# Expert results fetched and added on GpSimd inside the linear attention; scores of the gated heads in row groups

## The reference, cut to what matters

```
layer 0:  x += causal attention(16 heads of 64)
          x += cross attention(16 heads of 64, dense mask)
          t  = rmsnorm(layernorm(x)) * norm_weight
          x += layernorm(x) + sum over a token's two best of 8 experts of w_e * FFN_e(t)
layer 1:  x += linear attention: q, k = elu(qW)+1, elu(kW)+1; (sum of past k v^T) q / (sum of past k) q
          x += cross attention(16 heads of 16)
          x += gated heads:
               gates = sigmoid(x w_gate); of 8 experts per head only the best is kept (gm)
               values = einsum(gm, value_experts, x)
               out = softmax(causal(q k^T / 8)) values
               out = einsum(gm, output_experts, out), summed over 8 heads of 64
```

## Time and profile before

| | |
|---|---|
| median of 3 runs | 4053.97 us (4052.62 to 4055.01) |
| the profiled execution | 4053.33 us |
| its span, first to last instruction | 4051.5 us |
| TensorE busy | 3628.1 us (90%) |
| VectorE busy | 2985.8 us (74%) |
| ScalarE busy | 2128.6 us (53%) |
| GpSimd busy | 192.3 us (5%) |
| granted TensorE clock, mean | 0.956 of full speed |

### The profile page before, as it was taken

The page is one execution under the profiler, slowest core; times in us unless marked ns, Lnnn a source line. Parts: engine busy times, 40 slices in busy tenths (PEclk is TensorE's granted clock), DMA queues, the critical chain, the costliest instruction groups (busy, mean ns, idle before and its releaser), DMA issues. The chain is left out here.

```text
span 4051.5 us, 93201 instructions
## 1 busy us (share of the span) xinstructions
PE 3628.1 (90%) x28994; PEld 3057.7 (75%) x28994; DVE 2985.8 (74%) x9270; ACT 2128.6 (53%) x6632; POOL 192.3 (5%) x254
## 2 busy tenths in 40 slices
PE   6999999899999997099548879998799999999998
PEld 5888888688888887089436656665688888888887
DVE  5666666677777775556568868888888888888886
ACT  5777777677777773145213337776433333333333
POOL 0000000000000000611430000000000000000000
PEclk9999999899999996599879989999899999999999
DMA  2000000100000002522210000000200000000000
GB/s 96 0 0 0 0 0 0 58 11 10 11 15 10 10 6 99 171 72 77 78 52 0 0 19 21 19 17 16 93 13 13 10 10 13 8 10 13 10 11 9
DMA packets 56111, 109.74 MB, mean 27 GB/s; under 512 B 8368, under 2 KB 27184, under 8 KB 55728
## 3 DMA queue, kind: packets, MB, share of 16 engines
q1 hardware_dynamic: 46656, 80.72, 6.3%
q0 software_dynamic: 8464, 26.22, 2.0%
q10 hardware_dynamic: 864, 1.19, 0.1%
HBM read 72.46 MB, written 35.65 MB: 27 GB/s over the span
## 5 line engine op out<-in xcount | busy, mean ns | idle before, releaser
L637 ACT ACTIVATE c_pr<-c_sm,c_nmx 128x256 f32<-128x256 f32 x512 | 254.6, 499 | 153.6 <-DVE c_nmx L483 153.6
L2248 ACT CAST f_zgT<-f_ps_g 128x512 fp32r<-128x512 f32 x256 | 150.9, 590 | 319.7 <-PE f_ps_g L1977 319.7
L127 PE MATMUL f_ps_out<-f_out_rounded,f_zgT 128*128 128x256 f32 x1024 | 309.7, 302 | 0.0
L128 PE MATMUL f_ps_out<-f_out_rest,f_zgT 128*128 128x256 f32 x1024 | 287.9, 281 | 0.0
L129 PE MATMUL f_ps_out<-f_out_rounded,f_zgT 128*128 128x256 f32 x1024 | 287.6, 281 | 0.0
L637 ACT ACTIVATE a_pr<-a_sm,a_nmx 128x128 f32<-128x128 f32 (+1 forms) x512 | 227.1, 444 | 107.0 <-DVE a_nmx L483 107.0
L483 DVE CUSTOM_DVE_ANT_0 a_sm<-a_ps_s,causal 128x128 f32<-128x128 f32 (+1 forms) x512 | 152.6, 354 | 165.9 <-PE a_ps_s L369 165.9
L2097 DVE TENSOR_REDUCE f_v<-f_gv 128x64 f32<-128x512 f32 x256 | 269.3, 1052 | 0.4
L1700 ACT ACTIVATE c_pr<-c_ps_s,c_nmx 128x256 f32<-128x256 f32 x512 | 214.3, 500 | 89.7 <-DVE c_nmx L1551 89.7
L483 DVE CUSTOM_DVE_ANT_0 c_sm<-c_ps_s,c_mask 128x256 f32<-128x256 f32 x512 | 186.8, 421 | 92.1 <-PE c_ps_s L369 90.5
L2088 DVE TENSOR_TENSOR f_gv<-f_ps_v,f_gm_step 128x512 f32<-128x512 f32 x256 | 175.5, 686 | 97.9 <-PE f_ps_v L129 86.4
(11 more groups left out here) (368 smaller groups left out, 11309.3 us busy)
## 6 DMA issues: line engine op xcount, KB each, us to landing
f_slot_rows<-f_run POOLq DMA_DIRECT2D x1, 9216.0 KB, 34.9
f_rows<-f_slot_rows SPq DMA_DIRECT2D x72, 128.0 KB, 2.1
f_slot_out<-f_y SPq DMA_DIRECT2D x72, 128.0 KB, 1.9
c_ctx_stage<-in_ctxT SPq DMA_DIRECT2D x32, 256.0 KB, 2.8
small<-in_f_w SPq DMA_DIRECT2D x16, 512.0 KB, 3.9
x_sb<-in_x SPq DMA_DIRECT2D x8, 512.0 KB, 8.4
small<-in_c_w SPq DMA_DIRECT2D x8, 512.0 KB, 3.9
c_mask_stage<-in_mask SPq DMA_DIRECT2D x16, 256.0 KB, 3.0
```

Of the source, the lines that this page charges most:

```text
L127: nc.tensor.matmul(out, sh, mh, start=start, stop=False, **kw)
L128: nc.tensor.matmul(out, sh, ml, start=False, stop=False, **kw)
L637: last = nc.scalar.activation(pr[:, r, i, 0:n], sm[:, j, i, 0:n], ACT.Exp, bias=nmx[:, j, i:i + 1], scale=-1.0, accum_out=sums[:, r, i:i + 1])
```

## The change

Three things are changed. First, the gathers, the weighted additions and the statistics leave the end of the experts' block. In the linear attention GpSimd now fetches the results of one batch with four indirect DMAs, scales each with its weights and adds it to x, with eight operations of its own, batch by batch. VectorE measures batch b + 1 at the start of the first step of batch b, into small tiles of its own; ScalarE takes the root of that batch alone behind `apart` in that step, and then one exponential of a single column; VectorE inverts it ahead of `normalise(b + 1)`. The weights `wt` and the row numbers `slot_at` are kept beyond the experts' block. Second, the part below zero is taken by ScalarE as a Relu of the negative, ahead of its exponential, and `low_part` is gone. Third, in the gated heads q is scaled once, and the scores of the two heads of a step are products of 64 rows each, one in the upper and one in the lower half of the rows, alternating. They go to two banks, of which the second is `ps_qk`, the one of the projection, since all eight are in use. Both heads' scores now come at k = 1, the row maxima and exponentials at k = 1 and 2, the scaling at k = 2 and 3; `project` and the turn of x also wait for the maxima.

```diff
--- before.py
+++ after.py
...
-        wt = sb("wt", [P, TOPS, TILES])
-        slot_at = sb("slot_at", [P, TOPS, TILES], U32)
+        wt, slot_at = c.wt, c.slot_at
...
-        back = sb("back", [P, RR, TOPS, D])
...
-            all_stored(pool)
-            for n in range(TILES):
-                if n >= RR:
-                    pool.wait_ge(summed, n - RR + 1)
-                for r in range(TOPS):
-                    pool.indirect_dma_start(back[:, n % RR, r, :], None, c.y.rearrange("n p d -> (n p) d"),
-                                            bass.IndirectOffsetOnAxis(ap=slot_at[:, r, n:n + 1], axis=0)).then_inc(gathered[n % RR], 16)
...
-                nc.vector.tensor_scalar(xt(n), xt(n), grow[:, n:n + 1], move[:, n:n + 1], ALU.mult, ALU.subtract).then_inc(grown, 1)
+                nc.vector.tensor_scalar(xt(n), xt(n), grow[:, n:n + 1], move[:, n:n + 1], ALU.mult, ALU.subtract)
...
-            for n in range(TILES):
-                dve.wait_ge(gathered[n % RR], 16 * TOPS * (n // RR + 1))
-                dve.wait_ge(grown, n + 1)
-                nc.vector.scalar_tensor_tensor(xt(n), back[:, n % RR, 0, :], wt[:, 0, n:n + 1], xt(n), ALU.mult, ALU.add).then_inc(half_sum, 1)
-                dve.wait_ge(half_sum, n + 1)
-                nc.vector.scalar_tensor_tensor(xt(n), back[:, n % RR, 1, :], wt[:, 1, n:n + 1], xt(n), ALU.mult, ALU.add).then_inc(summed, 1)
-                if n % ST == ST - 1:
-                    dve.wait_ge(summed, n + 1)
-                    batch_stats(nc, dve, c, stats, n // ST)
...
+            fetched = sb("fetched", [P, ST, TOPS, D])
+            bn_in = sb("bn_in", [P, ST, 6])
+            mv_in = sb("mv_in", [P, ST, 2])
+            spare = sb("spare", [P, 1])
...
+                def fetch(b):
+                    for i in range(ST):
+                        if b:
+                            pool.wait_ge(summed, ST * (b - 1) + i + 1)
+                        for r in range(TOPS):
+                            pool.indirect_dma_start(fetched[:, i, r, :], None, c.y.rearrange("n p d -> (n p) d"),
+                                                    bass.IndirectOffsetOnAxis(ap=c.slot_at[:, r, b * ST + i:b * ST + i + 1], axis=0)
+                                                    ).then_inc(gathered[i], 16)
...
+                def add_experts(b):
...
+                    for i in range(ST):
+                        n = b * ST + i
+                        xt = c.x[:, n, :]
+                        pool.wait_ge(gathered[i], 16 * TOPS * (b + 1))
+                        for r in range(TOPS):
+                            nc.gpsimd.tensor_scalar(fetched[:, i, r, :], fetched[:, i, r, :], c.wt[:, r, n:n + 1], None,
+                                                    ALU.mult).then_inc(weighted, 1)
+                        pool.wait_ge(weighted, TOPS * n + 1)
+                        nc.gpsimd.tensor_tensor(xt, xt, fetched[:, i, 0, :], ALU.add).then_inc(half_sum, 1)
+                        pool.wait_ge(weighted, TOPS * n + 2)
+                        pool.wait_ge(half_sum, n + 1)
+                        nc.gpsimd.tensor_tensor(xt, xt, fetched[:, i, 1, :], ALU.add).then_inc(summed, 1)
+                for b in range(B):
+                    fetch(b)
+                    add_experts(b)
...
+            if softmax:
+                dve.wait_ge(root, 1)
+                nc.vector.reciprocal(rstd[:], rstd[:]).then_inc(root, 1)
+                dve.wait_ge(root, 2)
...
+            def measure(b):
+                dve.wait_ge(summed, ST * b + ST)
+                batch_stats(nc, dve, c, stats_in, b, bn_in, mv_in)
+            def invert(b):
+                at = rstd[:, bass.ds(b * ST, ST)]
+                dve.wait_ge(rooted, b + 1)
+                nc.vector.reciprocal(at, at).then_inc(inverted, 1)
             def normalise(b):
+                if not softmax:
+                    dve.wait_ge(inverted, b + 1)
...
-            def low_part(g, s, b):
-                n = 2 * b + s // 2
-                dve.wait_ge(proj, n + 1)
-                if late(g, 1):
-                    dve.wait_ge(qk_ready, n)
-                nc.vector.tensor_scalar(low[:], ps_p[:], 0.0, None, ALU.min).then_inc(phi_s, 1)
...
-                    if now and s % 2 == 0:
-                        low_part(*now)
+                    if s == 0 and (not isinstance(b, int) or b + 1 < B):
+                        measure(b + 1)
                     if ended:
                         finish(*ended)
                     for j in range(J):
...
                     if s == 3:
                         new_stats(b - 2)
                 if s == 1 and (not isinstance(b, int) or b + 1 < B):
+                    if not softmax:
+                        invert(b + 1)
                     normalise(b + 1)
+            if not softmax:
+                measure(0)
+                invert(0)
             normalise(0)
...
+            if softmax:
+                nc.scalar.activation(rstd[:], c.mv[:, :, 1:2].rearrange("p a d -> p (a d)"), ACT.Sqrt,
+                                     bias=c.eps[:]).then_inc(root, 1)
...
+            def take_root(b):
+                act.wait_ge(stats_in, 3 * b + 3)
+                nc.scalar.activation(rstd[:, bass.ds(b * ST, ST)],
+                                     c.mv[:, bass.ds(b * ST, ST), 1:2].rearrange("p a d -> p (a d)"), ACT.Sqrt,
+                                     bias=c.eps[:]).then_inc(rooted, 1)
+                nc.scalar.activation(spare[:], c.eps[:], ACT.Exp)
...
                 else:
+                    act.wait_ge(proj, n + 1)
+                    if late(g, 1):
+                        act.wait_ge(qk_ready, n)
+                    nc.scalar.activation(low[:], ps_p[:], ACT.Relu, scale=-1.0).then_inc(phi_s, 1)
                     act.wait_ge(phi_s, 2 * n + 1)
-                    nc.scalar.activation(low[:], low[:], ACT.Exp).then_inc(phi_s, 1)
+                    nc.scalar.activation(low[:], low[:], ACT.Exp, scale=-1.0).then_inc(phi_s, 1)
...
                 if not softmax and now:
                     apart(*now)
+                if not softmax and s == 0 and (not isinstance(b, int) or b + 1 < B):
+                    take_root(b + 1)
...
+            if not softmax:
+                take_root(0)
             take_xT(0)
             run_steps(act, STEPS, slot, LAST)
...
+        ps_s = [ps_s, ps_qk]
...
                 if late(b, 1):
                     pe.wait_ge(q_ready, STEPS * b)
+                    pe.wait_ge(maxed, 2 * STEPS * b - 2)
...
             def project(g, s):
                 if late(g, 1):
                     pe.wait_ge(q_ready, g)
+                if late(g, 2):
+                    pe.wait_ge(maxed, 2 * g - 2)
...
-            def scores(g, s, j):
-                pe.wait_ge(q_ready, g + 1)
-                if late(g, 1) or j:
-                    pe.wait_ge(maxed, 2 * g + j)
+            def scores(g, s, batches):
+                pe.wait_ge(q_ready, batches)
+                if late(g, 1):
+                    pe.wait_ge(maxed, 2 * g)
                 for i in range(ST):
-                    last = nc.tensor.matmul(ps_s[:, i * S:i * S + (i + 1) * P], qT[:, s % 2, j, i * P:(i + 1) * P],
-                                            kT[:, s % 2, 0:(i + 1) * P], start=True, stop=True)
-                last.then_inc(scored, 1)
+                    for j in range(2):
+                        rows = slice(64 * j, 64 * j + 64)
+                        last = nc.tensor.matmul(ps_s[j][:, i * S:i * S + (i + 1) * P], qT[rows, s % 2, i * P:(i + 1) * P],
+                                                kT[rows, s % 2, 0:(i + 1) * P], start=True, stop=True)
+                        if i == ST - 1:
+                            last.then_inc(scored, 1)
...
                 for k in range(K):
                     if now:
                         project_v(now[0], s, k, b)
-                    if k % 2 == 0 and one:
-                        scores(one[0], one[1], k // 2)
+                    if k == 1 and one:
+                        scores(one[0], one[1], now[0] + 1 if now else one[0] + 1)
                     if k % 2 and two:
                         turn(two[0], two[1], k // 2)
...
                         if k == 0:
                             cut_piece(now[0], s)
                         gate_v(now[0], s, k)
-                    if one and k % 2 == 0:
-                        row_max(one[0], one[1], k // 2)
+                    if one and k in (1, 2):
+                        row_max(one[0], one[1], k - 1)
                     if five:
                         rest_zgT(five[0], k)
                     if now:
                         sum_v(now[0], s, k)
-                    if one and k % 2:
-                        norm(one[0], one[1], k // 2)
+                    if one and k >= 2:
+                        norm(one[0], one[1], k - 2)
...
                 act.wait_ge(proj, g + 1)
                 if late(g, 2):
                     act.wait_ge(scored, 2 * g - 2)
```

(35 more changed lines are left out.)

11 lines of the change are left out of this document (6 added, 5 removed).

## The result

The changed kernel takes 4000.31 us (median of 4 runs, 3993.21 to 4004.44) against 4053.3 of the kernel before: a ratio of 0.987, with a 95% interval of 0.985 to 0.989. That is 53 us faster where 88 were forecast, and outside the range of 3946 to 3996. The profiled execution has a span of 4000.5 us.

The account below looks back on a forecast made before the run. Bounds: gather issue after the experts, a VectorE-TensorE loop of 19.17 us a batch in the linear attention, TensorE in the gated heads. 4051.5 - 84.5 + 12.6 + 12 - 28.2 = 3963.4 us of span, 3966 measured; range 3946 to 3996.

Parts of the forecast that it names:

- part 2: Linear attention's loop: VectorE gains the statistics and a reciprocal, loses low_part; 0.8 us a batch, +12 us over 15 batches.
- rival C: Linear attention grows more: table loads cost double (+15 us), or GpSimd slows VectorE by 10% (+14); 3981 us; chance 0.18.
- The start: Linear attention's first features come 22.5 us into the stage instead of 9.9, behind batch 1's statistics: 12.6 us given back.
- I take 0.6 for each of the eight: GpSimd's eight operations on 128x256 a batch in the linear attention: 0.6 us each, bounds 0.3 and 1.2.
- 6 us of a first call: GpSimd's first call after code is loaded takes about 6 us; one such call would add 6 us.
- The experts' end: Gathers leave the experts' block, so the linear attention starts at 1986.4 instead of 2070.9: 84.5 us off.
- Part 3: Gated heads' scores in row groups of 64: 60 steps gain 0.47 us each, 28.2 us; shared bank's waits eat nothing.
- TensorE gains 0.47 us a step: Gated heads: both heads' scores take 0.85 us a step instead of 1.32; bounds nothing and 0.66.
- The table loads: Linear attention, ScalarE's take_root: two loads of 1.28 us a batch, covered by its idle time, costed at nothing.
- B: Row groups bring nothing in the gated heads, through missing overlap or the shared bank's waits: 3994 us; chance 0.13.
- D: VectorE's extra 0.8 us vanishes in its wait, or row groups give 0.66: 3954 us, both 3943; chance 0.10.
- E: Slower: GpSimd paces the linear attention, other engines wait in measure; 4114 us at 3 us an operation; chance 0.04.

Follow-up runs that it names:

- filled_half_again: Changed kernel with five unread products a batch added on TensorE between scores and values of the first step, run again: 3978.52 us, ratio 0.982 to the kernel before.
- late_measure_again: Changed kernel with measure(b + 1) moved from ahead of finish to the first step's end, ScalarE's root behind its copy of v: 3955.78 us, run again 3956.60.
- late_no_additions_again: late_measure without GpSimd's weighting and additions, one column copied instead (experts' results missing from x), run again: 3940.84 us, ratio 0.973 to the kernel before.
- gated_only: Kernel before with only the gated heads' part of the change, scores of two heads in row groups: 4026.99 us, ratio 0.994.
- no_tables_again: Changed kernel with the root replaced by a Relu and no spare exponential, so no table loads in the loop, run again: 3999.01 us, ratio 0.987.
- second and third group of runs: Two of the five groups in which the kernels were run; kernels of one group share their chip and their runs of the kernel before.
- v_on_scalar: late_measure with the fill of v moved from VectorE to the end of ScalarE's step: 3979.01 us, ratio 0.979; run again 3948.60 us, 0.975.

## Why the prediction was wrong

**What failed** is the term "+12 us" of part 2, "0.8 us a batch". The loop lost 55.7 - 16.3 = 39.4 us beyond its later start, and not 12. For VectorE's work alone the size is right: with TensorE's clock held up, a batch is 19.96 us in filled_half_again, where 19.17 + 0.8 = 19.97 was worked out. Two things were missing in it. First, the step costed the later finish by VectorE's order only and never asked what a longer idle gap does to TensorE: the gap grew from 1.49 to 2.69 us and the clock fell behind it. filled_half_again prices that at 17 us. Second, the contention with GpSimd was not in the sum; it stood in rival C, as 14 us, and in the upper bound of 25 us, which didn't hold 39.4 either. In filled_half_again it is 21.0 - 19.96 = 1.0 us a batch beside GpSimd, some 8 us over eight batches. Between late_measure_again and late_no_additions_again it is 3956.60 - 3940.84 = 15.8 us, of which the features' start takes 4.8 (25.4 against 20.5 us into the stage), so 11. It falls on single instructions, the copies above all, not on all by a tenth. With both, 12 + 17 + 8 to 11 makes 37 to 40 us of the 39.4.

**The start**, 12.6 us forecast, was 16.3 (features at 26.2 instead of 9.9 into the stage). The mechanism, that the second measure holds the first features, was right. The term mis-sized is "I take 0.6 for each of the eight": they average (4 x 0.91 + 4 x 0.72) / 8 = 0.82, within the bounds of 0.3 and 1.2. The prediction's other estimate for the addition, 0.56 us, was low too, and the 6 us of a first call didn't show: the first two scalings took 1.84 us together and the next two 1.82.

**The experts' end**, 84.5 forecast, measured 85.1. Right.

**Part 3**, 28.2 forecast, measured 21.1 (gated_only 24 by its ratio, 19 to 30). The mechanism was right: the scores are 0.85 us and no wait for the shared bank took anything. The term mis-sized is "TensorE gains 0.47 us a step", which measured 0.36. It was read from the scores' own starts, and so left out the step into them: throughout the stage the scores start 0.33 us behind the value product, where they started 0.23 behind it, which is 0.10 of the missing 0.11. Why they start later is open.

**The table loads** and the Relu on ScalarE were costed at nothing, and no_tables_again shows nothing for the loads. A load took 1.28 us with the next operation right behind, so the drain of 1.38 us that the prediction weighs didn't show. Rival C's first half fell; its second was right in kind, and its 14 us were 8 to 11. Rivals B, D and E didn't come.

The sum with what was measured: 3966 + 17 for the clock, 8 to 11 for the contention, 4 for the start and 7 for part 3 is 4002 to 4005, against 4000.3.

## What to carry to other kernels

When an edit delays an engine that TensorE waits for, price the gap twice: once as time, and once as what the products behind it take if the clock falls. To see whether it fell, look for a product whose length you know and which now takes about double. Place added work where its engine already waits: the same measure cost nothing behind `fill_v` (19.17 - 1.21 + 0.25 = 18.21 us a batch without it, 18.23 with it) and 3.3 us a batch ahead of `finish` (21.5). When work is moved to GpSimd, look at what it does to VectorE: here GpSimd had time to spare, and the price was paid in VectorE's copies from SBUF to SBUF.

## What the runs showed of the hardware that was not expected

- TensorE's granted clock fell to 0.50 behind gaps of 2.69 us between batches in which it was busy otherwise, in some batches and not in others, in nearly all behind 3.36 us, and once in late_measure_again behind 1.84. Behind the 1.49 and 0.95 us of steady batches it stayed at 1.00. But the size of the gap alone doesn't decide: behind the 1.22 us of the stage's last batches `values` took 1.51 us in filled_half_again and 0.86 in the changed kernel, and 1.84 us left it at 0.86 twice in late_measure.
- On GpSimd a one-input scaling with a column of weights took 0.91 us for 128x256, a two-input addition 0.72, and a batch's four gathers 1.26 each as before.
- A second set of statistics right behind the first waited 0.64 us on "issue", where the instruction behind the single set of the kernel before waited 0.27.
- In the second and third group of runs the kernel before took 4059.6 and 4059.8 us instead of 4051 to 4053. In all seven profiles of these groups ScalarE's copy of z started late while GpSimd worked, with a releaser called "remote" that no profile of the other groups has; in v_on_scalar it did so about once behind each four gathers. There the last of four gathers is issued at 2096.56, `values` runs at 2094.86, and the copy comes only at 2098.52:

```profile
2098.52 0.37 ACT L1763 COPY l_zT<-l_ps_z 128x256 f32<-128x256 f32 x1 [5.85 <-remote]
```

The chip of the third group is that of the first, which shows none of this. The cause is open.
